# Layer 0's expert weights held in SBUF, experts stages of layers 1 and 3 written out tile by tile, four output buffers, early weights for layer 3

## What is computed

```
layer 0: top 2 of 8 experts, silu(x@gate)*(x@up) with 352 hidden columns, then @down;
         plus one shared expert of 704 columns
layer 1: top 1 of 8 experts, silu(x@W1 + b1) with 1024 hidden columns, then @W2 + b2
layer 2: two groups, each top 2 of 32 experts, 128 hidden columns, gated
layer 3: top 1 of 32 experts, 256 hidden columns, gated, at most 80 tokens per expert
```

## Time and profile before

| | us |
|---|---|
| median of 3 runs | 2632.03 (2630.26 to 2635.6) |
| the profiled execution, its own time | 2626.51 |
| span of the profiled execution | 2624.8 |
| TensorE busy | 2111.5 (80%) |
| VectorE busy | 1324.8 (50%) |
| ScalarE busy | 821.0 (31%) |
| GpSimd busy | 764.9 (29%) |

### The profile page before, as it was taken

How to read it: one execution, slowest core, us unless ns; L and a number is a source line. 1 busy time by engine, 2 the same in 40 slices (tenths; PEclk the granted TensorE clock), 3 DMA queues, 4 the chain that set the end, 5 groups by cost and what they waited for, 6 DMA issues and landing times. The chain is left out here.

```text
span 2624.8 us, 44700 instructions
## 1 busy us (share of the span) xinstructions
PE 2111.5 (80%) x14380; PEld 1732.9 (66%) x14380; DVE 1324.8 (50%) x3859; ACT 821.0 (31%) x1984; POOL 764.9 (29%) x1031
## 2 busy tenths in 40 slices
PE   6859997992899999998599948994893963787595
PEld 5746666981799989997588725663773842554484
DVE  3555521224688877885300065765435535675423
ACT  3602421212233333333232323452340432344221
POOL 1000002215344444443011032210446633232133
PEclk9869988995899999999699968996795986898697
DMA  2030008962211111100387534425467543441295
GB/s 77 9 124 16 1 0 312 319 206 87 80 41 39 36 33 41 37 20 7 149 308 299 190 106 127 127 79 225 111 134 275 162 107 104 115 122 47 91 327 167
DMA packets 147842, 318.82 MB, mean 121 GB/s; under 512 B 20752, under 2 KB 99856, under 8 KB 139344
## 3 DMA queue, kind: packets, MB, share of 16 engines
q1 hardware_dynamic: 130864, 270.64, 30.6%
q0 software_dynamic: 16800, 45.90, 7.0%
HBM read 257.09 MB, written 56.89 MB: 120 GB/s over the span
## 5 line engine op out<-in xcount | busy, mean ns | idle before, releaser
L1977 PEld LDWEIGHTS heads_ps_c<-heads_band,heads_sT 128*128 128x128 f32 x3072 | 363.0, 192 | 21.6 <-issue 17.5
L1977 PE MATMUL heads_ps_c<-heads_band,heads_sT 128*128 128x129 f32 x3072 | 368.2, 276 | 7.8 <-DVE heads_band L2195 7.5
L2133 POOL TENSOR_SCALAR heads_band<-heads_shifts,heads_taps 128x130 f32<-128x130 f32 x384 | 254.3, 677 | 268.1 <-PE heads_ps_c L1977 264.4
L2195 DVE SCALAR_TENSOR_TENSOR heads_band<-heads_shifts,heads_taps,heads_band 128x130 f32<-128x130 f32 x768 | 226.3, 350 | 32.4 <-POOL heads_band L2133 27.9
L2070 ACT ACTIVATE heads_probs<-heads_ps_c,heads_negmax 128x256 f32<-128x256 f32 x256 | 107.5, 471 | 370.5 <-DVE heads_negmax L2204 370.5
L1720 DVE TENSOR_REDUCE heads_negmax<-heads_ps_m 128x2 f32<-128x512 f32 x256 | 169.6, 688 | 80.2 <-PE heads_ps_m L1576 78.1
L1677 ACT ACTIVATE heads_probsT<-heads_ps_e 128x512 f32<-128x512 f32 x256 | 147.0, 596 | 194.4 <-PE heads_ps_e L1600 194.1
L953 DVE COPY experts_y<-experts_ps_y 128x256 f32<-128x256 f32 (+1 forms) x96 | 40.6, 423 | 302.3 <-PE experts_ps_y L879 205.1
L866 PE MATMUL experts_ps_g<-experts_xT,experts_w 128*128 128x128 f32 (+1 forms) x1504 | 190.2, 281 | 2.9 <-ACT experts_xT L908 2.9
L866 PEld LDWEIGHTS experts_ps_g<-experts_xT,experts_w 128*128 128x128 f32 x1504 | 181.3, 195 | 8.6 <-ACT experts_xT L908 5.8
L841 POOL COPY experts_x_ix<-token_of 128x1 uint32 x96 | 17.7, 185 | 579.0 <-PEq L851 338.7
(11 more groups left out here) (382 smaller groups left out, 4167.3 us busy)
## 6 DMA issues: line engine op xcount, KB each, us to landing
experts_w<-in_experts_dram SPq DMA_DIRECT2D x24, 2180.0 KB, 9.6
experts_w<-in_experts_dram SPq DMA_DIRECT2D x40, 1088.0 KB, 8.2
weights_w<-in_experts_dram SPq DMA_DIRECT2D x16, 1536.0 KB
experts_w<-in_experts_dram SPq DMA_DIRECT2D x32, 768.0 KB, 5.3
y_rows<-experts_y SPq DMA_DIRECT2D x190, 128.0 KB, 2.8
piece_rows<-heads_pieces SPq DMA_DIRECT2D x96, 192.0 KB, 2.7
heads_stackQ<-piece_rows SPq DMA_DIRECT2D x48, 192.0 KB
heads_stackK<-piece_rows SPq DMA_DIRECT2D x48, 192.0 KB
```

What stands on the lines that cost most here:

```text
L1977: last = pe.matmul(out[:, qc * SEQ + k0:qc * SEQ + k1], sT[:, h % 2, kc, qc * P + dq:qc * P + dq + P], band[:, h % 2, dq, w0:w0 + k1 - k0] ...
L2133: last = pool.tensor_scalar(band[:, h % 2, dq, :], shifts[:, 0, :], taps[:, r % 2, h, dq * TAPS:dq * TAPS + 1], None, ALU.mult)
L2195: last = v.scalar_tensor_tensor(out, shifts[:, d, :], taps[:, r % 2, h, tap:tap + 1], out, ALU.mult, ALU.add)
```

## The change

Layer 0's experts run in `resident_experts_stage` with all 8 experts (8.9 MB) loaded under `route0`, and this stage now comes ahead of the shared expert. NT becomes 39 for layer 0 and 23 for layer 1. `experts_stage` (layers 1 and 3) loses its loops, POOL's copy of the token numbers, and layer 1's bias matmul; it stores a tile before it loads the next weights. All experts stages have four output buffers. Layer 3's first 8 weights are loaded under `route3`. The core of the diff:

```diff
+YB = 4
-def experts_stage(..., biased=False, ahead=8):
+def experts_stage(..., biased=False, ahead=8,
+                  early=None):
-        w = s.sb("w", [P, ahead, W])
+        w = s.sb("w", [P, ahead, W]) if early is None else early.w
-        y = s.sb("y", [P, 2, D])
+        y = s.sb("y", [P, YB, D])
         def _(pool):
-            with pool.Fori(0, NT // ahead) as i:
-                for u in range(ahead):
-                    j = ahead * i + u
-                    pool.wait_ge(y_ready, j + 1)
-                    pool.tensor_copy(x_ix[:, u, :], tb.token_of[:, bass.ds(j, 1)]).then_inc(ix_ready, 1)
-                    pool.wait_ge(ix_ready, j + 1)
...
+            for j in range(NT):
+                if j >= ahead:
+                    pool.wait_ge(turned, j - ahead + 1)
+                pool.indirect_dma_start(xg[:, j % ahead, :], None, xn_dram,
+                                        bass.IndirectOffsetOnAxis(ap=tb.token_of[:, j:j + 1], axis=0))\
+                    .then_inc(x_in[j % ahead], 16)
+            def output_layer(j):
+                p, u = j % 2, j % ahead
+                pe.wait_ge(h_ready, j + 1)
+                if j >= 2:
+                    pe.wait_ge(y_copied, j - 1)
...
-                if biased:
-                    last = pe.matmul(ps_y[0:rows, p, 0:D], ones[0:1, 0:rows], b2(u), start=False, stop=True)
                 last.then_inc(y_ready, 1)
-            with pe.Fori(0, NT // ahead) as i:
-                for step in range(ahead + 2):
...
+            for step in range(NT + 2):
+                for lag, part in enumerate((turn_rows, hidden_layer, output_layer)):
+                    if 0 <= step - lag < NT:
+                        part(step - lag)
+            def copy_out(j):
+                p = j % 2
+                v.wait_ge(y_ready, j + 1)
+                if j >= YB:
+                    v.wait_ge(stored[j % YB], 16 * (j // YB))
+                if biased:
+                    v.tensor_tensor(y[0:rows, j % YB, :], ps_y[0:rows, p, 0:D], b2(j % ahead), ALU.add)\
+                        .then_inc(y_copied, 1)
+                else:
+                    v.tensor_copy(y[0:rows, j % YB, :], ps_y[0:rows, p, 0:D]).then_inc(y_copied, 1)
         def _(sp):
...
+            if early is None:
+                for j in range(ahead):
+                    load_weights(j)
+            for j in range(NT):
+                sp.wait_ge(y_copied, j + 1)
+                store(j)
+                if j + ahead < NT:
+                    load_weights(j + ahead)
+class InOrder:
+    def load(self, sp, j):
+        sp.dma_start(self.w[:, j % self.ahead, :], self.w_dram[j * P:(j + 1) * P, :])\
+            .then_inc(self.loaded[j % self.ahead], 16)
+    def load_first(self, sp):
+        for j in range(self.ahead):
+            self.load(sp, j)
...
 def resident_experts_stage(...):
-        y = s.sb("y", [P, 2, D])
+        y = s.sb("y", [P, YB, D])
...
 def build(...):
-        NT = TILES * 2 + 8
-        route_stage(core, "route0", logits[:, :, 0:8], 8, 2, NT, tb, ones, xn, xn_dram)
+        NT = TILES * 2 + 7
+        with Stage(core, "weights0") as weights:
+            resident = Resident(weights, 8, 2 * 2 * 352 + 3 * D)
+            route_stage(core, "route0", logits[:, :, 0:8], 8, 2, NT, tb, ones, xn, xn_dram,
+                        prefetch=lambda sp: resident.load(sp, i["experts0"]))
+            resident_experts_stage(core, "experts0", NT, [P, P, 96], resident, 1, tb, xn_dram, y_dram, ident, ones)
         kernels = core.keep("kernels", [P, B * HEADS * TAPS * TAPS])
         shared_kernels_stage(core, "shared0", ...)
-        experts_stage(core, "experts0", NT, P, [128, 128, 96], i["experts0"], tb, xn_dram, y_dram, ident, ones)
-        NT = TILES + 8
+        NT = TILES + 7
...
+        with Stage(core, "weights3") as weights:
+            in_order = InOrder(weights, i["experts3"], 8)
+            route_stage(core, "route3", logits[:, :, 0:32], 32, 1, 32, tb, ones, xn, xn_dram, capacity=CAP,
+                        prefetch=in_order.load_first)
+            experts_stage(core, "experts3", 32, CAP, [P, P], i["experts3"], tb, xn_dram, y_dram, ident, ones,
+                          early=in_order)
```

More of the change, by code:

```diff
@@ L795, in _, with experts_stage @@
             v.tensor_copy(tb.token_of[:, 0:NT], ps_tok[:, 0:NT])
[L798 removed]
+def experts_stage(core, name, NT, rows, chunks, w_dram, tb, xn_dram, y_dram, ident, ones, biased=False, ahead=8,
+                  early=None):
     F = sum(chunks)
@@ L882, in _ @@
-            with pe.Fori(0, NT // ahead) as i:
-                for step in range(ahead + 2):
-                    for lag, part in enumerate((turn_rows, hidden_layer, output_layer)):
-                        if 0 <= step - lag < ahead:
-                            part(i, step - lag)
+            def output_layer(j):
+                p, u = j % 2, j % ahead
+                pe.wait_ge(h_ready, j + 1)
+                if j >= 2:
+                    pe.wait_ge(y_copied, j - 1)
+                for f, m in enumerate(chunks):
+                    last = pe.matmul(ps_y[0:rows, p, 0:D], h[0:m, p, f, :], down_w(u)[0:m, f, :],
+                                     start=(f == 0), stop=(f == NF - 1))
+                last.then_inc(y_ready, 1)
@@ L962, in _ @@
+            for step in range(NT + 1):
+                if step < NT and not biased:
+                    multiply(step)
+                if step >= 1:
+                    copy_out(step - 1)
         @block.sync
         def _(sp):
[L964 to L974 removed]
@@ L976, in store @@
-            def store(i, u):
-                j = ahead * i + u
-                sp.wait_ge(y_copied, j + 3)
-                sp.dma_start(y_dram[dyn(j, rows), :], y[0:rows, u % 2, :]).then_inc(stored[u % 2], 16)
-            for u in range(ahead):
-                load_weights(0, u)
-            with sp.Fori(1, NT // ahead) as i:
-                for u in range(ahead):
-                    load_weights(i, u)
-                    store(i - 1, u)
-            for u in range(ahead):
-                store(NT // ahead - 1, u)
@@ L989, in _, with load_weights, store @@
-            for p in range(2):
-                sp.wait_ge(stored[p], 16 * (NT // 2 + 1))
+            def load_weights(j):
+                if early is not None:
+                    early.load(sp, j)
+                    return
+                row = sp.value_load(tb.weights_of[0:1, j:j + 1], min_val=0, max_val=w_dram.shape[0] - P)
+                sp.dma_start(w[:, j % ahead, :], w_dram[bass.ds(row, P), :]).then_inc(w_in[j % ahead], 16)
+            def store(j):
+                sp.dma_start(y_dram[j * rows:(j + 1) * rows, :], y[0:rows, j % YB, :])\
+                    .then_inc(stored[j % YB], 16)
```

130 lines of the change are left out of this document (53 added, 77 removed).

## The result

The changed kernel takes 2564.67 us (median of 4 runs, 2561.07 to 2569.23) against 2631.15 (4 runs, 2626.55 to 2635.6): ratio 0.975, 95% interval 0.9731 to 0.9768. The forecast of 2564 us and its sign hold. The profiled execution took 2561.07 us (span 2559.4), 65.4 less than the one before with its 2626.5.

The account below looks back on a forecast made before the run. TensorE bounds the changed stages, with DMA second. Savings of -11.9 - 34.1 - 8.5 - 13.6 = -68.1 us take the profiled 2626.5 to 2558.4, plus 5.5 gives a 2564 us median; range 2549 to 2580, chance 0.75.

Parts of the forecast that it names:

- Layer 0: Layer 0's experts: start 3.8 us, 39 tiles of 4.22, rest for clock and ends; 177.9 against 189.8, -11.9 us.
- turning the roles round: Layer 0's tile: swapping roles of rows and weights saves no TensorE time, 4.22 us against 4.18; three new turns eat it.
- Layer 1: Layer 1's experts: 23 tiles of 7.2 us plus opening and end; 183.1 against 217.2, -34.1 us.
- weights keep up: Layer 1's weight loads: 2.49 MB per 7.2 us tile needs 346 GB/s; TensorE sets the pace with 5% to spare.
- 366 at a full share: Layer 1's DMA rate: 304 GB/s at share 0.83 means 366 GB/s when full, so a tile's traffic needs 6.8 us.
- The DMA rival: Layers 1 and 3: weights become the bound; up to 2588 us in total, likelier 2576; chance 0.19.
- Layer 2: Layer 2's two groups: four output buffers recover two thirds of 6.3 us lost per group, 4.3 each, -8.5 us.
- the bound of -12.6: Layer 2's two groups: the far limit of the gain from four buffers, -12.6 us; the other limit was 0.
- Layer 3: Layer 3's experts: start 3.8 us, 32 tiles of 2.83, early loads hidden; 102.7 against 116.3, -13.6 us.
- The move of the shared expert's stage: Shared expert's stage placed behind layer 0's experts: costs nothing, between -2 and +3 us for the clock it finds.
- Unrolled code: Written-out experts stages: cost nothing; should instruction fetching stall, at most 2 us a stage.
- Slower: Layer 0's experts: gaps from single-buffered `ps_h` and `ps_y` halve the clock, up to +165 us, 2729; chance 0.04.

Follow-up runs that it names:

- the spread gathers: Changed kernel with two output buffers, unused lanes gathering the row of their own lane number, not row 0: layer 2's groups took 121.1 and 122.0 us.

## Why the prediction was right

- **Layer 0**: forecast 177.9 us, -11.9; measured 178.0. The start (3.8, measured 4.2) and the tile (4.22, measured 4.21) hold, and turning the roles round saves no TensorE time: the old roles, run in the same way, give the same stage. What I had not said is what follows from it: all of the 11.8 could be had without residency, and without the 2.4 us that residency and the new order cost in layer 1's projection.
- **Layer 1**: forecast 183.1, -34.1; measured 185.6, -31.6. The term that was mis-sized is the tile, 7.2 for 7.25 (23 x 0.05 = 1.2); the other 1.3 lies in opening and end, where one wait for weights of 1.8 us stands that I had not counted. The bias is worth 23 x 0.77 = 17.7 us, not "some 20".
- **The condition "weights keep up"** held with far more to spare than the 5% of the text. The estimate "366 at a full share" was wrong: dividing a rate by the share it was measured at gave 366, and 399 GB/s were kept up. The nearest row, 407 GB/s in the opening, was the right one to go by. The DMA rival at 0.19 had no ground up to 399 GB/s.
- **Layer 2**: forecast -8.5 for both groups, measured 5.5 + 7.0 = 12.5 and, by undoing it alone, 12.8. The mis-sized term is the share of the loss that four buffers recover. I took two thirds of it without a reason for that share; it was all, the bound of -12.6. What the spread gathers show is that the gathers of the unused tiles are slow, not the queue as such. That four buffers are enough to cover these is measured; why they are is not shown.
- **Layer 3**: forecast 102.7, -13.6; measured 103.6, -12.7. The pace of 2.83 and the hidden cost of the early loads hold; the start is 4.3, not 3.8.
- **The move of the shared expert's stage**: costed at nothing, bounds -2 and +3; measured +2.9. The forecast named a stage that leaves 236 us as a sign of being wrong, and on this point it was. Layer 1's projection, costed at nothing as untouched, +2.7. The first goes with a longer time at half clock and not with the order, since both lengths occur in either place; what sets the clock's course is open. The second comes with the resident stage and its place: 38.9 us only where these are undone. A lower granted clock (0.82 over the stage, 0.85 and 0.86 in the short ones) is all that the rows show of its cause.
- **Unrolled code**: costed at nothing. In the first profile nothing speaks against it. No experiment takes it alone, and the cause of the long step in layer 2's opening on the other chips (the stage is some 6 us longer, over the bound of 2) is open; layer 2 was written out before the change too.
- **Slower** had 0.04: `ps_h` and `ps_y` with one buffer left TensorE busy 168.7 of the stage's 178.0 us, and the clock over layer 0's stage is 0.97.

The total is off by less than a microsecond because errors cancel, and that closeness is luck: measured against forecast, layer 1 +2.5, layer 3 +0.9, layer 2 -4.0, layer 0 +0.1, outside the experts +3.2, together 2.7. The profiled execution lies 3.6 us below its median where the one before lay 5.5 below the median that the forecast used, which takes 1.9 off again.

## What to carry to other kernels

Take the price of a part from undoing that part alone: the part that names a change, here weights kept in SBUF, can be worth nothing while a bias of one row is worth 17.7 us and two small buffers 12.8. Where TensorE sets the pace, look in its weight loads for "idle before" around odd-shaped matmuls and give such work to an engine that already touches the data. And where padding is gathered, don't let it all read one row; the DMA share then rises while GB/s fall, which is the sign to look for.

## What the runs showed of the hardware

- Gathers in which all lanes read the same row are slow: with them 129 GB/s at a share of 0.84, with distinct rows 163 GB/s at 0.52 in like stretches late in the stage; their packets took 676 to 954 ns where those of distinct rows took 169 to 345.
- A core alone kept 399 GB/s over 80 us with a pace of TensorE that did not change, though the share of the DMA engines was 0.94 already at 349 GB/s.
- A one-row float32 matmul of 256 columns costs 0.77 us between 128-row ones, a 128-row one 0.43.
- On the chips of the experiments three combining stages, layer 2's groups and the route between them took 2.5 to 8.5 us longer each, and the experts of layers 0, 1 and 3 did not: the same code took 1.6% longer there (2604.86 against 2564.67 us).
